# Four graph layers on one core: layer 2's split features turned by DMA and prepared with three f16 products

## What is computed

```python
h = relu(layernorm(x)); x = x + L0(h, adj)      # attention over neighbours
h = relu(layernorm(x)); x = x + L1(h, adj)      # (adj @ h + beta*h) / deg @ kernel + bias
h = relu(layernorm(x)); x = x + L2(h, adj)      # relu(D^-1/2 (adj+I) D^-1/2 @ (h @ W) + b)
h = relu(layernorm(x)); x = x + L3(h, adj)

def L3(x, adj):                                  # hyperbolic layer; x is h
    h = h_add(exp0(log0(x) @ embed), embed_bias)
    neigh = exp0(adj @ log0(h))
    out = exp0(log0(concat(x, neigh)) @ layer)
    return h_add(out, layer_bias)
```

## Time and profile before

| | us |
|---|---|
| median of 3 runs | 905.12 (904.7 to 905.52) |
| the profiled execution, its own time | 904.95 |
| its span in the profile | 903.2 |
| TensorE busy | 849.7 (94%) |
| VectorE busy | 626.5 (69%) |
| ScalarE busy | 487.1 (54%) |
| GpSimd busy | 289.5 (32%) |

### The profile page before, as it was taken

One profiled execution on the slowest core, in us unless ns is written; L12 is line 12 of the kernel. 1 busy time (PEld: TensorE's weight loads), 2 busy tenths in 40 slices (PEclk: granted clock), 3 DMA queues, 4 the chain that ended last, 5 costly groups with the idle time before them and its releaser, 6 DMA issues.

```text
span 903.2 us, 18349 instructions
## 1 busy us (share of the span) xinstructions
PE 849.7 (94%) x6464; PEld 510.3 (57%) x6464; DVE 626.5 (69%) x1775; ACT 487.1 (54%) x1027; POOL 289.5 (32%) x381
## 2 busy tenths in 40 slices
PE   0699999999999999999999999999999999999992
PEld 0366777777777777654444455555455555555451
DVE  6989999999999999953444313313147676637776
ACT  5878888888888886731222111111055566434543
POOL 6844444444654464531221100000022131213221
PEclk9999999999999999999999999999999999999997
DMA  8999999999999994000000000000000000000000
GB/s 262 223 224 271 234 269 232 282 232 254 258 271 249 240 249 111 2 1 1 1 1 0 1 1 1 1 1 1 1 1 1 1 1 1 1 1 25 24 24 25
DMA packets 96080, 89.79 MB, mean 99 GB/s; under 512 B 74368, under 2 KB 79616, under 8 KB 96000
## 3 DMA queue, kind: packets, MB, share of 16 engines
q1 hardware_dynamic: 92352, 88.11, 41.2%
q10 hardware_dynamic: 3648, 0.61, 0.4%
HBM read 69.81 MB, written 2.10 MB: 80 GB/s over the span
## 4 chain that ended last, share of the span: by engine, by line
PE 70%; DVE 15%; issue 6%; ACT 3%; DVEq 2%; POOL 2%; DMA 1%; ACTq 1%; SPq 0%; POOLq 0%
PE ps_acc L1353 28%; PE ps_acc L1264 16%; PE ps_s L1247 10%; PE ps_t L1353 6%; PE ps_t L1247 5%; DVE e_parts L803 2%; DVE ps_s L796 2%; POOL att_sb L385 1%; ACT e_parts L612 1%; DVE adj_t L735 1%; PE ps_s L1383 1%; PE ps_s L1415 1%; DMA x<-in_x 1%; PE ps_acc L1341 1%; ACT ez L571 1%
## 5 line engine op out<-in xcount | busy, mean ns | idle before, releaser
L334 POOL CAST e_parts<-ez 128x512 f16<-128x512 f32 x256 | 158.2, 645 | 177.5 <-ACT ez L483 116.1
L1264 PEld LDWEIGHTS ps_acc<-h_a,e_parts 128*128 128x128 f16 x3072 | 185.8, 97 | 34.4 <-DVE e_parts L803 4.2
L1264 PE MATMUL ps_acc<-h_a,e_parts 128*128 128x129 f16 x3072 | 197.4, 219 | 2.5 <-DVE e_parts L803 2.3
L1353 PE MATMUL ps_acc<-adj_t,stage 128*128 128x512 fp8e4 x896 | 198.6, 379 | 0.0
L803 DVE TENSOR_TENSOR e_parts<-ez,e_parts 128x512 f16<-128x512 f32 x256 | 180.0, 744 | 1.0 <-POOL e_parts L334 1.0
L1353 PE MATMUL ps_acc<-adj_t,h_a 128*128 128x512 fp8e4 x768 | 170.3, 379 | 0.0
L1353 PEld LDWEIGHTS ps_acc<-adj_t,stage 128*128 128x128 f16 x896 | 87.1, 98 | 99.1
L1247 PE MATMUL ps_s<-u_t 128*128 128x512 f16 x534 | 132.3, 385 | 9.0 <-ACT ez L483 7.3
L458 ACT ACTIVATE bytes<-stage 128x1024 uint8<-128x1024 f32 x128 | 133.8, 1046 | 0.9 <-DVE x L764 0.7
L483 ACT ACTIVATE ez<-ps_s,scal 128x1024 f32<-128x1024 f32 x89 | 107.1, 1203 | 44.4 <-DVE ps_s L796 43.3
L571 ACT ACTIVATE ez<-x,small 128x128 f32 (+1 forms) x96 | 39.6, 482 | 155.4 <-DVE small L980 155.4
(11 more groups left out here) (157 smaller groups left out, 814.4 us busy)
## 6 DMA issues: line engine op xcount, KB each, us to landing
stage<-in_adj SPq DMA_DIRECT2D x128, 512.0 KB, 5.0
x<-in_x SPq DMA_DIRECT2D x4, 512.0 KB, 8.5
adj_t<-bytes SPq DMA_TRANSPOSE x128, 5.1
out<-x SPq DMA_DIRECT2D x8, 256.0 KB, 2.2
kernel_sb<-in_L_gnn_kernel ACTq DMA_DIRECT2D x1, 64.0 KB, 7.1
w_sb<-in_L_gnn_W ACTq DMA_DIRECT2D x1, 64.0 KB, 8.1
embed_top<-in_L_gnn_embed ACTq DMA_DIRECT2D x1, 64.0 KB, 8.4
embed_top<-in_L_gnn_layer ACTq DMA_DIRECT2D x1, 64.0 KB, 7.3
```

Of the source, the lines that this page charges most:

```text
L334: g.tensor_copy(e_parts[:, HI, at, :], ez[:, at, :]).then_inc(ehi_done, 1)
L1264: last = t.matmul(att_acc[:, b, 0:D + 1], e_parts[:, re, g_s % RING, P * b:P * (b + 1)], h_a[:, s, rh, 0:D + 1], start=(s == 0 and n == 0 ...
L1353: last = t.matmul(acc, h[:, k, r, :], adj_f8[:, k // 2, CW * c:CW * (c + 1), k % 2], start=(k == 0 and r == LO), stop=(k == NB - 1 and r = ...
```

## The change

The features' parts are no longer turned by TensorE. SyncE, in the middle of its program, waits for each `split_h(2, m)` and issues two transposing DMAs (two blocks each, high and low part) from `hs` to a new tile `ht` of f16, which takes the place of `ht_sb`. `turn_h`, `ht_evac` and their semaphores are gone. `prepare` makes three f16 products for each block (high x high, high x low, low x high) with a matrix `embed16`, split into two f16 parts by two VectorE operations ahead of layer 0's last steps; it waits for the DMAs, and for the last hw evacuation of the chunk before. `prep_evac` undoes the scales. `split_h(2, m)` waits until the transposes of chunk m-1 have landed. `prepare` stands after 23, 27, 39, 43, 55, 59, 71, 75. In layer 3's list two more quarters of chunk 3 come ahead of the last quarters of chunks 0 to 2, without the wait for ht_evac, and the steps w(0) to w(5) stand after 26, 28, 36, 38, 44, 50.

```diff
+W_SCALE = 64.0
 QUARTERS_3 = ([(c, q) for q4 in ((0, 1, 2, 3), (4, 5)) for c in (0, 1, 2) for q in q4]
-              + [(3, q) for q in range(4)] + [(c, q) for c in (0, 1, 2) for q in (6, 7)]
-              + [(3, q) for q in range(4, 8)]
+              + [(3, q) for q in range(6)] + [(c, q) for c in (0, 1, 2, 3) for q in (6, 7)]
               + [(c, q) for c in range(4, NCH) for q in range(8)])
-W_AFTER = (W_0, W_1, [15, 20, 29, 35, 46, 51, 61, 67], [24, 26, 33, 35, 42, 49, 57, 64])
-T_AFTER = ((), (), [20, 25, 37, 41, 53, 57, 69, 73], ())
-V_AFTER = tuple([t + 1 for t in ts] for ts in T_AFTER)
+W_AFTER = (W_0, W_1, [15, 20, 29, 35, 46, 51, 61, 67], [26, 28, 36, 38, 44, 50, 57, 64])
+V_AFTER = ((), (), [23, 27, 39, 43, 55, 59, 71, 75], ())
...
-        ht_sb = bytes8[:, 1, :].bitcast(F32)
+        ht = bytes8[:, 1, :].bitcast(F16).rearrange("p (b r i) -> p b r i", b=BC, r=2)
...
+            for m in range(NCH):
+
+                sp.wait_ge(l_split, NCH * 2 + m + 2)
+                if m:
+                    sp.wait_ge(prep_done, m)
+                for n in range(2):
+                    sp.dma_start_transpose(
+                        ht[:, 2 * n:2 * n + 2, :, :].rearrange("p b r i -> p (b r) i")
+                        .bitcast(U16),
+                        hs[:, 2 * n:2 * n + 2, :, :].rearrange("p b r f -> p (b r f)")
+                        .bitcast(U16)).then_inc(ht_in, 16)
...
-            def ht_evac(at):
-                act.wait_ge(ht_ps, at + 1)
-                a.activation(ht_sb, ps_t[:, 0, :], ACT.Copy, scale=1.0 / H_SCALE
-                             ).then_inc(ht_out, 1)
...
             def prep_evac(m, par):
 
                 act.wait_ge(prep_done, m + 1)
-                a.activation(v0[:, BC * par:BC * (par + 1), :], prep_out2[:, :, 0, :], ACT.Copy
-                             ).then_inc(v_out, 1)
+                back = 1.0 / (H_SCALE * W_SCALE)
+                a.activation(v0[:, BC * par:BC * (par + 1), :], prep_out2[:, :, 0, :], ACT.Copy,
+                             scale=back).then_inc(v_out, 1)
...
+            v.tensor_scalar(embed16[:, HI, :, :], embed_top[:, :, :], W_SCALE, None, ALU.mult)
             v.tensor_scalar(beta2, l1b, A_VALUE, None, ALU.mult)
             dve.drain()
+            v.scalar_tensor_tensor(embed16[:, LO, :, :], embed_top[:, :, :], W_SCALE,
+                                   embed16[:, HI, :, :], ALU.mult, ALU.subtract
+                                   ).then_inc(embed_ok, 1)
...
-            def split_h(L, m):
+            def split_h(L, m, first=False):
 
                 dve.wait_ge(l_relu, NCH * L + m + 1)
+                if L == 2 and not first:
+                    dve.wait_ge(ht_in, 32 * m)
...
-                        elif c == 3:
-                            pe.wait_ge(ht_out, NCH)
...
-            def turn_h(L, m):
-
-                pe.wait_ge(l_split, NCH * L + m + 2)
+            def prepare(L, m):
+
+                pe.wait_ge(ht_in, 32 * (m + 1))
+                if m == 0:
+                    pe.wait_ge(embed_ok, 1)
+                else:
+                    pe.wait_ge(hw_out, m)
                 for b in range(BC):
-                    for r in (LO, HI):
-                        last = t.matmul(ps_t[:, 0, P * b:P * (b + 1)], hs[:, b, r, :], ident16[:, :],
-                                        start=(r == LO), stop=(r == HI))
-                last.then_inc(ht_ps, 1)
-
-            def prepare(L, m):
-
-                pe.wait_ge(ht_out, m + 1)
-                for b in range(BC):
-                    last = t.matmul(prep_out2[:, b, :, :], ht_sb[:, P * b:P * (b + 1)],
-                                    embed_top[:, :, :], start=True, stop=True)
+                    for n, (rh, rw) in enumerate(((HI, HI), (HI, LO), (LO, HI))):
+                        last = t.matmul(prep_out2[:, b, :, :], ht[:, b, rh, :],
+                                        embed16[:, rw, :, :], start=(n == 0), stop=(n == 2))
                 last.then_inc(prep_done, 1)
```

More of the change, by code:

```diff
@@ L162, in program @@
             hyp[:, n, :] for n in range(26))
+        embed16 = att_sb[:, :, :].rearrange("p b f -> p (b f)")[:, 26 * PB:26 * PB + 2 * D].bitcast(
+            F16).rearrange("p (r a f) -> p r a f", r=2, a=2)
         ps_s = ctx.enter_context(nc.psum_tensor("ps_s", [P, 4, CW], F32))
@@ L204, in program @@
                  "pow_in pow_ok hd_sum hd_hi hd_ok agg_done agg_out agg_turned w_done l_stats "
-                 "l_rstd l_scale l_relu l_split ht_ps ht_out prep_done bias_in hw_out x_done "
+                 "l_rstd l_scale l_relu l_split ht_in embed_ok prep_done bias_in hw_out x_done "
                  "h_sq_in n_h_ok v_sq_in n_v_ok h2_sq_in n_h2_ok a_sq_in n_a_ok cat_sq_in "
@@ L215, in program @@
          pow_in, pow_ok, hd_sum, hd_hi, hd_ok, agg_done, agg_out, agg_turned, w_done, l_stats,
-         l_rstd, l_scale, l_relu, l_split, ht_ps, ht_out, prep_done, bias_in, hw_out, x_done,
+         l_rstd, l_scale, l_relu, l_split, ht_in, embed_ok, prep_done, bias_in, hw_out, x_done,
          h_sq_in, n_h_ok, v_sq_in, n_v_ok, h2_sq_in, n_h2_ok, a_sq_in, n_a_ok, cat_sq_in,
@@ L622, in prep_evac @@
                 act.wait_ge(prep_done, m + 1)
-                a.activation(v0[:, BC * par:BC * (par + 1), :], prep_out2[:, :, 0, :], ACT.Copy
-                             ).then_inc(v_out, 1)
+                back = 1.0 / (H_SCALE * W_SCALE)
+                a.activation(v0[:, BC * par:BC * (par + 1), :], prep_out2[:, :, 0, :], ACT.Copy,
+                             scale=back).then_inc(v_out, 1)
                 squares(lambda b: prep_out2[:, b, 0, :],
-                        lambda b: v_sq[:, BC * par + b:BC * par + b + 1]).then_inc(v_sq_in, 1)
-                a.activation(hw[:, ds(BC * m, BC), :], prep_out2[:, :, 1, :], ACT.Copy
-                             ).then_inc(hw_out, 1)
+                        lambda b: v_sq[:, BC * par + b:BC * par + b + 1],
+                        scale=back).then_inc(v_sq_in, 1)
+                a.activation(hw[:, ds(BC * m, BC), :], prep_out2[:, :, 1, :], ACT.Copy,
+                             scale=back).then_inc(hw_out, 1)
             def ln_step(k, cut=PAIR):
@@ L649, in _ @@
             agg_evac(2 * NCH + 1, ps_acc[:, 1, :])
-            ht_evac(0)
             relu_chunk(1, 2 * NCH + 1)
@@ L655, in _ @@
                 m = 2 * i + 2
-                ht_evac(m - 1)
                 ln_step(2 * i + 1)
@@ L665, in _ @@
                 squares_h(m)
-                ht_evac(m)
                 relu_chunk(m + 1, 2 * NCH + m + 1)
@@ L670, in _ @@
             i = NCH // 2 - 1
-            ht_evac(NCH - 1)
             ln_step(2 * i + 1)
@@ L1141, in _ @@
                 norm_scale(2, m)
-                split_h(2, m)
+                split_h(2, m, m == 0)
             with dve.Fori(0, NCH // 2 - 1) as i:
@@ L1400, in weights @@
                 last.then_inc(w_done, 1)
-            def turn_h(L, m):
-                pe.wait_ge(l_split, NCH * L + m + 2)
-                for b in range(BC):
-                    for r in (LO, HI):
-                        last = t.matmul(ps_t[:, 0, P * b:P * (b + 1)], hs[:, b, r, :], ident16[:, :],
-                                        start=(r == LO), stop=(r == HI))
-                last.then_inc(ht_ps, 1)
-            def prepare(L, m):
-                pe.wait_ge(ht_out, m + 1)
-                for b in range(BC):
-                    last = t.matmul(prep_out2[:, b, :, :], ht_sb[:, P * b:P * (b + 1)],
-                                    embed_top[:, :, :], start=True, stop=True)
+            def prepare(L, m):
[4 more added lines that the diff above has]
+                    pe.wait_ge(hw_out, m)
+                for b in range(BC):
+                    for n, (rh, rw) in enumerate(((HI, HI), (HI, LO), (LO, HI))):
+                        last = t.matmul(prep_out2[:, b, :, :], ht[:, b, rh, :],
+                                        embed16[:, rw, :, :], start=(n == 0), stop=(n == 2))
                 last.then_inc(prep_done, 1)
             def small_steps(L, idx):
-                for steps, after in ((weights, W_AFTER), (turn_h, T_AFTER), (prepare, V_AFTER)):
+                for steps, after in ((weights, W_AFTER), (prepare, V_AFTER)):
                     for m, at in enumerate(after[L]):
```

## The result

| kernel | median, us | ratio to the kernel before, 95% interval |
|---|---|---|
| before, in the same comparison | 905.43 | |
| after | 908.33 (907.5 to 909.12) | 1.0033 [1.0023, 1.0043] |

The change made the kernel 2.9 us slower. The profiled execution of the kernel after took 907.5 us, with a span of 905.7 where I had worked out 902.9. So the trace has to account for 2.8 us.

A forecast was written before the change was run, and what follows sets the result against it. A dependent chain over VectorE, GpSimd and ScalarE, nearly level with TensorE, was taken as the bound: 7.0 us of saved TensorE work return as waits, 0.3 us remain, 905.12 becomes 904.8 us; range 901.5 to 909.0.

The forecast's parts named there:

- the likeliest case: Whole kernel: the dependent chain over VectorE, GpSimd and ScalarE sets the time; 904.4 to 906.5 us, 4 in 10.
- L of 3.7: Layer 2: from the end of a chunk's split until both its transposes are in, 3.7 us.
- Part 5: Layer 3: VectorE's second pair starts 1.41 us later, the last chunk 0.3 us earlier than before.
- Part 2: Layer 2: DMA transposes replace TensorE's turns, data in 3.7 us after the split; bounds 3.6 and 6.4.
- rival (b): Layer 2: transposes land later than in the quiet rows, preparations wait; costs 1.9 us or more, 3 in 10.
- Rival (c): Layer 3's w(5): the clock falls during TensorE's wait, 1.7 us lost, time 906.4 us; 1 in 10.
- the 4.5 us of waits: Layer 3: TensorE's new waits at w(4) and w(5) together, in two parts each shorter than 5.56 us.
- the range: Whole kernel: measured time between 901.5 and 909.0 us, leaving out 2 in 10.
- the Sum: Whole kernel: 7.0 us of TensorE's work go but come back as waits; span 903.2 becomes 902.9.

The follow-up runs named there:

- placed: Changed kernel with other positions for preparations and layer 2's and 3's steps, layer 3's quarters as in the kernel before: 900.39 us, ratio 0.9947 to the kernel before.
- fill_w5: Changed kernel plus 12 dead matmuls of 512 columns right ahead of layer 3's w(5): 906.15 us, ratio 1.0011 to the kernel before.
- shift_fetch: Changed kernel plus forty dead products of 16 columns on TensorE near the start: 907.01 us, ratio 1.0021 to the kernel before.

## Why the prediction was wrong, point by point

**What was right.** The mechanism: the likeliest case, that the chain sets the time, holds. w(2) waited 0.95 us (1.1 worked out), prep(3) came within 0.02 us, prep(7) waits 0.24 us (0.33), TensorE's saved work is hidden behind waits. f16 products of 256 columns, priced at 1.31 us for twelve on a line between two rows, gave 1.31: the quarter after prep(1) follows at 678.01. The transposes' L of 3.7 held at chunks 1 to 3 and 5 to 7. That layer 3's later steps give back layer 2's gain was in Part 5, and taking them back gave 903.65 us.

**Where the forecast failed.** Two terms were taken as nil that are not.
- Part 2 took one L for all eight chunks, from "the queues are idle in this stage". The windows gave the DMA engines almost nothing to do, and almost is the point: the queue of instruction fetches, which the profile's page lists, was not among the rows that I read. One such packet among chunk 4's cost 0.9 us at prep(4), and nothing behind it made up for it, just as rival (b) says of any excess. Rival (b) had the mechanism, but with crowded queues as its reason, a delay of all chunks, and not of one.
- Rival (c) had the place and nearly the price: 1.7 us for 1.4 measured. Its chance, 1 in 10, was mis-sized. I argued that each part of the 4.5 us of waits is shorter than the 5.56 us of the earlier trace rows; but that row shows that 5.56 us suffice, not that less does not. A wait of 1.14 us left the clock at 1.00, one of 1.67 in `placed` too, and one of 2.86 did not. The Trainium skill (TensorE: Matmul & The Clock Gate, Why this matters for your kernels) warns of idle gaps in the middle of a kernel; the runs agree with it and it should have weighed more.

Together 1.2 + 1.4 us are the 2.6 of the table (0.9 of the 1.2 is shown to be the fetch's; the rest is spread over several steps); the remaining 0.2 of the span's 2.8 lie behind w(7) and were not followed up. Without the two the span would be near 903.1, as before; no run takes both away. Taken away alone, the clock's fall left a ratio of 1.0011 (`fill_w5`) and the fetch 1.0021 (`shift_fetch`), about what 0.2% allows: the two cases were priced as alternatives and came together. 908.33 lies below the 909.0 of the range, but that end came from a landing late for all chunks, not from this sum: that it lies inside is luck. The waits that the Sum lists come to 8.2 us for 7.0 of work; the kernel before already waited 0.9 us at w(5) of layer 3, and the forecast was added up step by step, so nothing hangs on that list.

**The profiled execution and the median.** 907.5 us is the lowest of the eight runs, and the median is 0.8 above it. The second profile of the same kernel (own time 908.16) enters layer 2 0.37 us later, its prep(4) waits 0.17 longer, and its step from w(5) to w(6) is 0.08 longer: 0.62 of the 0.66 us between the two are so accounted for.

## What to carry to other kernels

When an edit takes work from an engine that runs level with a dependent chain, the gain exists only where the steps on that chain move earlier: here the same transposes and products gave +2.9 us with steps moved later and -4.8 us with steps placed by the chain. Here a wait of 2.9 us in front of TensorE had a second price, the slower clock behind it; dead products in it cost nothing and bought 1.4 us. Of two rare mishaps, also price both at once, and after taking a wait away, work out the next one before counting the gain.

## What was not expected of the hardware

- A 16 KB instruction fetch occupied one DMA engine for 0.93 us, and the last two packets of a transpose came only when it ended: landing 4.3 us where 2.4 is usual. It met chunk 4 in both traced executions of the kernel after; forty short products on TensorE 700 us earlier moved it away (from 735.8 to 730.2 us), so its place goes by TensorE's program.
- The granted clock fell to 0.50 after an idle stretch of 2.86 us between bursts at full clock, and w(5) paid for it; waits of 0.9 to 1.67 us left it at 1.00.
- The clock at the start differs between executions of one kernel: from 30 to 50 us it was 0.84 and 0.99 in the first profile of the kernel after, 0.71 and 0.95 in the second, which entered layer 2 0.37 us later.
